# A new order of the same calls on four engines, with 32 more identity transpositions ahead of the first token tiles' work

## What is computed

```
x  [4, 256, 128]                 1024 tokens
1) x = x + attn(layernorm(x))    w_qkv [128, 384]; q and k rms-normed and times ln_w;
                                 16 heads of 8, causal softmax within groups of 32 tokens;
                                 w_proj [128, 128]
2) x = x + xattn(layernorm(x), ctx)
                                 layernorm(gamma, beta); w_q [128, 1024]; ctx [4, 64, 128];
                                 w_kv [128, 2048]; 16 heads of 64, softmax over the 64 context
                                 rows; w_out [1024, 128], b_out; times tanh(gate)
3) x = x + moe(layernorm(x))     router [16, 128] -> sigmoid scores + bias; 2 of 4 groups by
                                 their best two; 4 of 16 experts by top_k; weights normed, x 2.5
                                 each expert: (silu(x Wg) * (x Wu)) Wd, all 128 x 128;
                                 plus 2 shared experts without weights
```

## Time and profile before

| | us |
|---|---|
| median of 3 runs | 195.54 |
| lowest, highest run | 192.97, 196.81 |
| the profiled execution, its own time | 196.71 |
| its span, first to last instruction | 195.20 |
| TensorE busy (matmul) | 177.7 |
| DVE busy | 145.9 |
| POOL busy | 121.7 |
| ACT busy | 116.2 |
| mean granted clock of TensorE | 0.965 |

### The profile page before, as it was taken

One profiled execution on the slowest core, in us unless ns is written; L12 is line 12 of the kernel. 1 busy time (PEld: TensorE's weight loads), 2 busy tenths in 40 slices (PEclk: granted clock), 3 DMA queues, 4 the chain that ended last, 5 costly groups with the idle time before them and its releaser, 6 DMA issues.

```text
span 195.2 us, 4807 instructions
## 1 busy us (share of the span) xinstructions
PE 177.7 (91%) x1671; PEld 127.9 (66%) x1671; DVE 145.9 (75%) x296; ACT 116.2 (60%) x276; POOL 121.7 (62%) x190
## 2 busy tenths in 40 slices
PE   5579999999878999999999989997997999999984
PEld 5345666666545657877787757455765888888863
DVE  2636387868877888888899876999999566756841
ACT  2344778677776678866778677153624663663640
POOL 4726234625671866887978766983966665746670
PEclk9855799999999999999999999999999999999999
DMA  4667000000007029200000006462330066443301
GB/s 121 168 230 200 3 0 7 5 3 3 0 27 195 0 77 291 67 3 2 0 0 3 0 7 199 149 217 72 126 104 0 7 218 178 175 130 108 111 0 54
DMA packets 16983, 15.92 MB, mean 82 GB/s; under 512 B 1841, under 2 KB 12609, under 8 KB 16833
## 3 DMA queue, kind: packets, MB, share of 16 engines
q1 hardware_dynamic: 16672, 15.49, 26.3%
q10 hardware_dynamic: 288, 0.13, 0.2%
HBM read 15.03 MB, written 0.59 MB: 80 GB/s over the span
## 4 chain that ended last, share of the span: by engine, by line
PE 63%; DVE 14%; DMA 6%; issue 5%; ACT 5%; POOL 2%; SPq 2%; DVEq 0%; ACTq 0%; POOLq 0%
PE wide L1771 8%; PE bank L1799 6%; PE wide L1829 5%; PE wide L1830 5%; PE wide L1831 5%; PE bank L1716 4%; DMA wkv_sb<-w_rows 3%; PE bank L1870 3%; PE bank L1871 3%; PE bank L1873 3%; PE wide L1731 3%; DMA wq_sb<-in_L_xattn_w_q_dram 2%; PE bank L1625 2%; PE bank L1785 2%; DVE vbd L1398 2%
## 5 line engine op out<-in xcount | busy, mean ns | idle before, releaser
L627 POOL TENSOR_TENSOR aw_lo<-vbd,aw_hi 128x512 fp32r<-128x512 f32 x26 | 33.4, 1295 | 20.3 <-ACT aw_hi L902 20.1
L886 ACT ACTIVATE kbd<-wide 128x512 f32<-128x512 f32 x36 | 21.4, 598 | 27.2 <-DVE wide L1387 16.3
L1829 PE MATMUL wide<-x3hi,gu_lo 128*128 128x512 f32 x72 | 31.4, 436 | 2.2 <-DVE vbd L1398 1.5
L1830 PE MATMUL wide<-x3lo,gu_hi 128*128 128x512 f32 x72 | 28.6, 397 | 0.0
L1831 PE MATMUL wide<-x3hi,gu_hi 128*128 128x512 f32 x72 | 28.3, 393 | 0.0
L1387 DVE TENSOR_TENSOR wide<-kbd,wide 128x512 f32<-128x512 f32 x27 | 18.5, 689 | 10.6 <-PE wide L1831 7.4
L902 ACT CAST aw_hi<-vbd 128x512 fp32r<-128x512 f32 x26 | 15.8, 617 | 6.4 <-DVE vbd L1398 4.3
L1398 DVE TENSOR_TENSOR vbd<-wide,wkv_sb 128x512 f32<-128x512 f32 x27 | 18.5, 689 | 1.3 <-DMA wkv_sb<-w_rows 0.6
L1829 PEld LDWEIGHTS wide<-x3hi,gu_lo 128*128 128x128 f32 x72 | 13.5, 188 | 8.2 <-issue 3.6
L515 POOL TENSOR_TENSOR p<-p,rs 128x1024 f32<-128x1024 f32 x8 | 15.2, 1903 | 3.6 <-DVE rs L1239 3.6
L1799 PE MATMUL bank<-vo_fold,p2T 128*128 128x128 f32 x128 | 16.7, 280 | 0.5 <-DVE x L1245 0.4
(11 more groups left out here) (176 smaller groups left out, 416.2 us busy)
## 6 DMA issues: line engine op xcount, KB each, us to landing
wkv_sb<-w_rows SPq DMA_DIRECT2D x32, 256.0 KB, 3.2
wkv_sb<-in_L_xattn_w_kv_dram SPq DMA_DIRECT2D x1, 1024.0 KB, 4.8
kv<-in_L_ffn_gate_w_dram SPq DMA_DIRECT2D x4, 256.0 KB, 4.2
kv<-in_L_ffn_up_w_dram SPq DMA_DIRECT2D x4, 256.0 KB, 5.2
wq_sb<-in_L_xattn_w_q_dram SPq DMA_DIRECT2D x1, 512.0 KB, 4.6
wout_sb<-in_L_xattn_w_out_dram SPq DMA_DIRECT2D x1, 512.0 KB, 6.5
wq_sb<-in_L_ffn_down_w_dram SPq DMA_DIRECT2D x1, 512.0 KB, 3.8
wqT<-in_L_ffn_down_w_dram SPq DMA_DIRECT2D x1, 512.0 KB, 5.1
```

Of the source, the lines that this page charges most:

```text
L627: pool.tensor_tensor(aw_lo[:, k % 3, :], weighted_of(k), aw_hi[:, k % 3, :].bitcast(F32), ALU.subtract).then_inc(alo_s, 1)
L886: sc.activation(sil[:, k % 2, :], bank[up_bank(k)], ACT.Silu).then_inc(sil_s, 1)
L1829: pe.matmul(dst, lo, x3hi[:, cols], start=True, stop=False)
L1830: pe.matmul(dst, hi, x3lo[:, cols], start=False, stop=False)
```

## The change

All calls of before stand in the lists of after, each as often as before: 122 calls on POOL, 234 on ACT, 193 on DVE, and 282 on TensorE, with six keep_busy calls added there, which are 2 + 9 + 9 + 6 + 3 + 3 = 32 transpositions. WIDE_TURNS follows TensorE's new order. SyncE's list and all functions are the same. The diff is cut to the parts that are spoken of; in the others neighbours change places in the same way.

TensorE:

```diff
             keep_busy(12)
             transpose_xn(0, 0, T1[:, 0:P])
+            keep_busy(2)
             project_v(0)
             fold(("ctx", 0))
             project_qkv(0)
+            keep_busy(9)
             fold(("wq", 0), halves=(0,))
             fold(("wq", 0), halves=(1,))
+            keep_busy(9)
+            transpose_qk(0)
             fold(("wq", 1))
-            transpose_qk(0)
+            keep_busy(6)
             transpose_xn(0, 1, T1[:, 0:P])
+            keep_busy(3)
             project_qkv(1)
+            scores1(0)
             project_v(1)
-            scores1(0)
             fold(("kv", 0), halves=(0,))
             fold(("kv", 0), halves=(1,))
+            keep_busy(3)
             transpose_qk(1)
             fold_A(0)
             transpose_xn(0, 2, T1[:, 0:P])
             fold(("kv", 1), halves=(0,))
+            fold(("kv", 1), halves=(1,))
             project_qkv(2)
+            scores1(1)
             project_v(2)
             transpose_p1(0)
-            scores1(1)
-            fold(("kv", 1), halves=(1,))
...
             fold_A(7)
-            values1(6)
+            fold_VW(0)
+            project_y(6)
             scores2(0)
-            project_y(6)
             transpose_p1(7)
-            fold_VW(0)
...
             transpose_p2(5, 0)
             scores2(7)
-            transpose_xn(2, 3, T1[:, P:2 * P])
+            gate(0)
             transpose_p2(5, 1)
             logits(3)
+            up(0)
             output2(5, 0)
+            gate(1)
             output2(5, 1)
             transpose_p2(6, 0)
-            gate(0)
-            up(0)
+            up(1)
+            transpose_xn(2, 4, T1[:, P:2 * P])
             transpose_p2(6, 1)
+            logits(4)
+            down(0)
```

ACT:

```diff
             squares(0)
+            scale_qk(0)
             copy_fold(("wq", 0))
-            scale_qk(0)
             copy_qkT(0)
             copy_xnT(1)
+            squares(1)
             copy_fold(("wq", 1))
-            squares(1)
-            gate_tanh()
             scale_qk(1)
...
             copy_p2T(5, 0)
-            copy_x3T(3)
-            split_hi(12)
+            silu(0)
             copy_p2T(5, 1)
             exp_logits(3)
             exp2(7)
             copy_p2T(6, 0)
-            silu(0)
-            split_hi(13)
-            copy_p2T(6, 1)
-            silu(1)
             split_down_hi(0)
             copy_x3T(4)
+            split_hi(10)
+            split_down_hi(1)
+            copy_p2T(6, 1)
+            exp_logits(4)
+            silu(1)
             copy_p2T(7, 0)
+            copy_x3T(5)
+            copy_p2T(7, 1)
             silu(2)
-            exp_logits(4)
-            copy_p2T(7, 1)
-            split_hi(14)
-            copy_x3T(5)
             exp_logits(5)
```

DVE:

```diff
+            zero_vbd()
             norm_stats(0, 0)
             norm_stats(0, 1)
             norm_apply(0, 0)
-            zero_vbd()
+            head_mask()
             norm_stats(0, 2)
             norm_stats(0, 3)
+            norm_apply(0, 1)
+            build_vbd(0)
             norm_stats(0, 4)
...
             softmax2_sub(7)
-            residual2(5)
+            multiply(0)
             biased_scores(0)
             softmax2_sum(7)
+            residual2(5)
+            norm_stats(2, 5)
             group_scores(0)
-            norm_stats(2, 5)
-            multiply(0)
+            residual2(6)
+            norm_stats(2, 6)
             rank_groups(0)
...
             biased_scores(1)
+            group_scores(1)
             multiply(3)
             multiply(4)
-            group_scores(1)
+            rank_groups(1)
             multiply(5)
             weigh(2)
...
             multiply(9)
-            rank_groups(1)
             weigh(9)
```

POOL:

```diff
             build_kbd(0)
-            late_constants()
...
-            scale_bias()
...
-            add_bias()
...
+            norm_apply(1, 4)
+            norm_p2(0)
+            late_constants()
+            scale_bias()
+            norm_scale(1, 6, 1.0 + LN_EPS, LN_EPS * LN_EPS)
             add_bias()
-            norm_scale(1, 4, 1.0 + LN_EPS, LN_EPS * LN_EPS)
-            norm_apply(1, 3)
-            norm_scale(1, 5, 1.0 + LN_EPS, LN_EPS * LN_EPS)
-            norm_scale(1, 6, 1.0 + LN_EPS, LN_EPS * LN_EPS)
             norm_scale(1, 7, 1.0 + LN_EPS, LN_EPS * LN_EPS)
-            norm_p2(0)
...
```

More of the change, by code:

```diff
@@ L672, in _ @@
+            norm_p2(3)
             norm_scale(2, 1, 1.0, LN_EPS)
+            norm_apply(2, 1)
+            split_lo(2)
             norm_apply(1, 6)
-            norm_apply(2, 1)
-            norm_p2(3)
             split_x3(0)
-            norm_p2(4)
             norm_scale(2, 2, 1.0, LN_EPS)
             norm_apply(2, 2)
+            norm_p2(4)
             norm_apply(1, 7)
             split_x3(1)
+            norm_scale(2, 3, 1.0, LN_EPS)
+            norm_apply(2, 3)
             norm_p2(5)
-            norm_scale(2, 3, 1.0, LN_EPS)
@@ L1108, in _ @@
             copy_rows(1)
[L1109 removed]
+            split_act_hi(17)
             silu(20)
[L1111 removed]
             split_act_hi(18)
+            silu(21)
             copy_y(0)
+            silu(22)
             split_act_hi(19)
[L1115 removed]
             split_act_hi(20)
[L1117 removed]
             silu(23)
@@ L1122, in _ @@
             silu(25)
+            silu(26)
             split_act_hi(23)
-            silu(26)
+            silu(27)
             split_act_hi(24)
@@ L1536, in _ @@
             weigh(5)
+            multiply(7)
             weigh(6)
-            multiply(7)
             weigh(7)
@@ L1546, in _ @@
             weigh(10)
+            mask_groups(1)
             multiply(11)
             weigh(11)
-            mask_groups(1)
             multiply(12)
+            choose_experts(1)
+            weigh(12)
             multiply(13)
-            weigh(12)
             weigh(13)
-            choose_experts(1)
             multiply(14)
+            multiply(15)
+            weigh(14)
             chosen_scores(1)
-            weigh(14)
-            multiply(15)
+            multiply(16)
             weigh(15)
-            multiply(16)
+            weigh(16)
             expert_weights(1)
-            weigh(16)
             multiply(17)
@@ L1569, in _ @@
             multiply(21)
+            multiply(22)
             weigh(21)
             add_y()
-            multiply(22)
             weigh(22)
@@ L1922, in _ @@
             fold(("kv", 1), halves=(0,))
+            fold(("kv", 1), halves=(1,))
             project_qkv(2)
+            scores1(1)
             project_v(2)
             transpose_p1(0)
-            scores1(1)
-            fold(("kv", 1), halves=(1,))
+            fold_A(1)
+            fold(("kv", 2), halves=(0,))
             values1(0)
             transpose_qk(2)
-            fold(("kv", 2), halves=(0,))
+            fold(("kv", 2), halves=(1,))
+            transpose_xn(0, 3, T1[:, 0:P])
             project_y(0)
-            transpose_xn(0, 3, T1[:, 0:P])
-            fold_A(1)
+            transpose_p1(1)
             project_qkv(3)
@@ L2089, in _ @@
             up(5)
+            gate(7)
+            gate(8)
             up(6)
-            gate(7)
             up(7)
-            gate(8)
             down(2)
@@ L2101, in _ @@
             up(9)
+            down(6)
+            up(10)
             gate(11)
-            down(6)
             gate(12)
-            up(10)
+            up(11)
             down(7)
-            up(11)
+            up(12)
+            gate(13)
             down(8)
-            gate(13)
-            up(12)
+            gate(14)
             up(13)
-            gate(14)
             down(9)
@@ L2115, in _ @@
             up(14)
+            down(10)
+            up(15)
             gate(16)
-            down(10)
             down(11)
-            gate(17)
-            up(15)
-            gate(18)
             down(12)
@@ L2182, in _ @@
             down(33)
+            gate(35)
             down(34)
```

432 lines of the change are left out of this document (211 added, 221 removed), and 6 rows, old and new, of the table WIDE_TURNS.

## The result

The changed kernel takes **193.71 us** (median of 11 runs, 193.12 to 194.76) against 195.54 (192.97 to 196.81) for the kernel before in the same comparison. The ratio is 0.994, with a 95% interval from 0.9912 to 0.9968: faster by 0.6%, or some 1.2 us. The ratio leaves out as slow the three runs of before that took over 1.5% more than its fastest (195.92, 196.46 and 196.81 us); the two medians alone are 1.8 us apart, and what follows goes by ratios. The forecast was 192.5 us, 3.0 us or 1.6% less than before. The sign is right and the time lies in the range, but of the 3.0 us the ratio shows 1.2.

The account below looks back on a forecast made before the run. TensorE was taken to bound most of the kernel, with a half-clock dip in the head, and DVE from 99 to 150 us. Sum: 196.71 - 3.8 - 0.6 + 1.3 - 1.1 = 192.5 us, range 189.0 to 197.0.

Parts of the forecast that it names:

- Together -3.8 us: TensorE's head: transpositions keep the clock full; fold_A(0) 2.4 us earlier, 1.4 us more up to the kv 1 half.
- the walk: New order of the head followed at warm durations from the wq transpositions at 8.40 us to fold_A(0) at about 16.0.
- Perhaps the quick run kept its clock: Guess that the 192.97 us run of before held full clock; runs differ by 3.8 us, the clock term's worth.
- the clock falls all the same: Rival: half clock from 8.4 to 22 us, dummies cost 3.2 us and give nothing back; 199.5 us, chance 0.12.
- zero_vbd() at the head: DVE's head: first tile's norm 0.1 to 0.4 us later, hidden by the wq DMA; taken 0.
- The fold order: Around 57 us: fold_VW(0) ahead of scores2(0) fills TensorE's idle gaps; -0.6 us, bounds 0 and -1.1.
- POOL's bias: add_bias behind norm_p2(0), ready before output2(0) with 0.5 to 2.5 us cover; taken 0, bounds 0 and +0.5.
- ACT's tables: Five exp/silu switches instead of three, exp2(7) 3.2 us and routing 2.4 us late; +1.3 us, bounds 0 and +3.8.
- The second routing: rank_groups(1) moved into DVE's wait for the weight rows before 121.12 us; -1.1 us, bounds 0 and -3.3.
- the order is worth more: Rival: filled waits in the DVE-bound stretch give their upper bounds, loads half hidden; 189.2 us, chance 0.26.

Follow-up runs that it names:

- the head alone: New order with the 32 transpositions up to about 78 us, the order of before from there, against before: 1.004, median 196.34 us.
- the execution above with 1.0: Profiled execution of before with only group_scores(1) moved ahead of multiply(3) and rank_groups(1) ahead of multiply(5); timed at 0.9951 of before, median 194.31 us.
- The head without the 32: New order without the 32 transpositions up to about 78 us, the order of before from there, against before: 1.0017, median 195.96 us.
- the tail alone: Order of before without new transpositions up to about 78 us, the new order from there, against before: 0.9963, median 194.22 us.
- the one move in before: Before with group_scores(1) moved ahead of multiply(3) and rank_groups(1) ahead of multiply(5) on DVE, against before: 0.9951, median 194.31 us.
- one more call in DVE's wait: Changed kernel without the 32 transpositions, with mask_groups(1) moved right behind rank_groups(1), against before: 0.9839, median 192.23 us.

## Why the prediction was right or wrong

**The clock and the 32 transpositions: the step that failed.** It is the line "Together -3.8 us". That the 32 would hold the clock was right in all four executions that have them. But the lead at the mark was 1.98 us and not 3.8 (1.6 in the mean of all executions), and the timed kernels keep nothing of it that can be measured: 0.994 with the transpositions and 0.9934 without, 1.0017 for the new head without them and 1.004 with them. Three things were wrong in it.

The first is that a lead in the head was taken for time at the end. In the head alone, with the 32, the walk came true: fold_A(0) started at 16.05 us and the lead at the mark was 2.44 us. It was still 2.46 us at the second store of weight rows, 0.62 us at the loads behind it and 0.6 us at the end (below: "What gave lead back later").

The second is the base. I took 196.71 us, the profiled execution, for my sum, though "the median of the runs is 195.54, 1.2 less than the profiled one" stands in it, and I put the difference down to the clock term instead of taking it off. The lead of 0.6 us against a trace that was 1.2 us slow is how the head alone can come out at 1.004. I can't say how long the timed runs of before were at half clock in the head. Before was timed 87 times beside the experiments, with mean granted clocks from 0.965 (6 runs, median 196.66 us) over 0.974 (15, 195.75), 0.982 (11, 194.56) and 0.991 (13, 194.44) to 1.0 (37, 195.27), and 5 runs with other values. But the execution above with 1.0 had a cold head up to 21.9 us, and the changed kernel's 0.991 comes from a dip at 112 us: the mean doesn't tell of the head. Of these, the two lowest clocks go with the slowest runs, the highest doesn't go with the fastest. "Perhaps the quick run kept its clock" isn't borne out, and isn't settled either.

The third is the walk's start, in the changed kernel. It gave the nine behind project_qkv(0) 1.0 us and put their end at 7.75, ahead of the wq DMA. They ran from 8.16 at the half pace and ended at 9.9, so the wq transpositions began 1.5 us later than in the earlier trace rows, and 2.4 later than in the execution with the old head and the new tail. Fillers that are meant to keep an engine warm are part of a queue: where it is cold nevertheless they cost double, in front of the work they should help. That this isn't the whole of it the head alone shows, whose nine ran at 0.11 us apiece.

**The rival "the clock falls all the same".** Its condition didn't come (the clock was full from 9.71 us in the stretch of 8.4 to 22 that decides it), and neither did its price. A rule of the Trainium skill had spoken for it ("TensorE: Matmul & The Clock Gate", Part 4: PE-mode transpose, the full clock doesn't engage for transposes). The runs don't bear it out as a rule: the twelve identity transpositions from 2 us were the only work before full clock at 4.79 us in the execution with the new head alone; in before it came at 4.91, with the transposition of tile 0 from 4.76 besides. They aren't a reliable trigger either: with the same twelve, the clock rose only at 9.71 in the changed kernel and at 18.20 with the old head and the new tail. What decides it isn't shown by any run here.

**zero_vbd() at the head.** Taken: 0. The transposition of tile 0 came at 5.41 us where it was 4.76: 0.65 us late, and not 0.1 to 0.4. project_qkv(0) came at 7.31 for 6.16, but 0.55 of these 1.15 us aren't zero_vbd's: in the head alone, with the same zero_vbd() and the 32 and a clock at full, it came at 6.76. It's one reason why the nine started only at 8.16. Whether it costs time in the end stays open (0.989 with it moved back, overlapping).

**The fold order.** Taken: -0.6. The head without the 32, which has it, doesn't beat before (1.0017). No run isolates the move of fold_VW(0); nothing shows the 0.6, and 0 is nearer.

**POOL's bias.** Taken: 0, and right: add_bias starts at 67.77 and ends at 69.03, output2(0, 0) starts at 71.21. The cover is 2.2 us, in the range of 0.5 to 2.5.

**ACT's tables.** Taken: +1.3. There are five loads, as said, and the tail alone loses 1.9 us up to the last routing step and 1.1 at the weight rows. The size holds, but not by the path I gave: exp2(7) started at 97.69 us against 98.88, which is 0.8 us late against the lead of 1.98 and not 3.2, and the routing began at 97.83 against 99.32, 0.5 us late and not 2.4 (1.4 in the tail alone). That the loads alone are the loser is argued, since other neighbours changed there too; the experiment that was to price them changed TensorE's waits instead.

**The second routing.** Taken: -1.1. Two measurements isolate it: 0.49% from the one move in before (1.0 us), and 0.69% between the new order without the 32 with and without it (0.9934 against 1.0003, 1.3 us). The term was right, the waits it named moved as said, and it is the whole of the measured gain: without it (and without the 32) the ratio is 1.0003.

**What gave lead back later.** The changed kernel stores the second set of weight rows 4.16 us earlier than the trace of before, and then DVE waits 3.43 us for their loads (155.55), where before waited 0.56. At the end 3.1 us of lead are left. SyncE's DMA queue shows it, in before, in the changed kernel and in the one with the new head alone:

```profile
152.67 1.72 SPq L447 DMA_DIRECT2D w_rows<-w_rows_sb  x4
...
155.43 1.76 SPq L441 DMA_DIRECT2D wkv_sb<-w_rows  x4
```

```profile
148.51 2.57 SPq L447 DMA_DIRECT2D w_rows<-w_rows_sb  x4
...
152.12 1.76 SPq L441 DMA_DIRECT2D wkv_sb<-w_rows  x4
```

```profile
150.21 1.71 SPq L447 DMA_DIRECT2D w_rows<-w_rows_sb  x4
...
154.81 1.77 SPq L441 DMA_DIRECT2D wkv_sb<-w_rows  x4
```

From the first store to the first load it was 2.76 us in before, 3.61 in the changed kernel and 4.60 with the new head alone: a store 2.46 us earlier gave loads only 0.62 us earlier. That is where most of its 2.44 us of lead at the mark went; the old order with the 32 lost 0.90 us in the same place (3.66 us).

What the record shows beside it is a packet of the DMA queue that the profile calls "instruction", 16 KB and about 1 us long. DMA queues of the new head alone from 152.4 to 153.8 us, and of before from 152.6 to 157.2, all of its stretch from store to load:

```profile
q8 instruction: 1, 0.02, 5.5%
q1 hardware_dynamic: 32, 0.01, 3.3%
```

```profile
q1 hardware_dynamic: 195, 0.17, 12.7%
```

5.5% of 16 engines in 1.4 us are 1.2 us of one of them. The slowest store took 3.3 us to land there, and 1.9 in before. In all four executions with the 32 such a packet starts between the first store of these rows and their last load (149.7 to 152.5 us), and each loses 0.85 to 1.84 us there: three between store and load, the fourth (zero_vbd() moved back) in the loads, which take 2.68 us where they took 1.76. In the nine usable ones without the 32 it starts only after these loads (157.3 us or later) and nothing is lost. So added instructions seem to shift the moment at which the program's own code is loaded, here onto the store that matters. That the packet is the cause is argued from this coincidence; no run moved it alone.

**The rival "the order is worth more".** It named the right stretch, and the change didn't reach it. With one more call in DVE's wait, and without the 32, the time is 192.23 us. That this is near the forecast of 192.5 is luck: it comes by another way than the forecast took.

## What to carry to other kernels

Before a stall in one trace gets a price, look at the same stretch in other executions, and by the pace of the instructions: a mean granted clock of 1.0 hid a cold head here. A lead at an early mark isn't time yet; follow it to the places where engines meet, since instructions added at the head can move something else, here, it seems, the code's own loading. A chain of tiny steps on the engine that sets the pace belongs into a wait of that engine: two moved calls gave 0.5%. A third gave nothing in the old order (0.9952 after 0.9951), where POOL was busy beside it, and 1% in the new one (0.9839 after 0.9934), where POOL was idle; that POOL makes the difference is likely from the step lengths, not isolated. Fillers for the clock stand in the queue ahead of real work; count them at the slow pace.

## What the runs showed of the hardware

**Tiny DVE steps last as long as POOL's instruction beside them.** cmp_a (128x64) took 1.31 us from 130.75 in before and ended at 132.06. The timeline of POOL in before has

```profile
130.65 1.33 POOL L627 TENSOR_TENSOR aw_lo<-vbd,aw_hi 128x512 fp32r<-128x512 f32 x1 [0.95 <-ACT aw_hi L902]
```

which ends at 131.98. A pair of 0.92 and 1.29 us was shown above (ends 119.51 and 119.48). With POOL idle the same forms take 0.22 and 0.17. The Trainium skill, "SBUF — State Buffer", Who interferes with whom, says that a DVE instruction with two SBUF inputs contends with a GpSimd instruction that reads SBUF, that the shared ports are an exclusive lock, and that the order of issue decides who blocks. cmp_a has two inputs in SBUF and started 0.10 us behind POOL's instruction, and in both pairs the ends lie less than 0.1 us apart, as this says; the step of 0.92 us has one, and for tensor_scalar the same section names a mode of its own that takes both ports, which no row here shows. I had read the 1.31 us as the step's own length; beside an idle POOL it takes 1.1 us less.

**The clock of TensorE isn't the same from run to run.** One order of instructions gave mean granted clocks from 0.965 to 1.0, and one timed run of the new head alone had 0.858 and took 204.53 us, where its others took 194.92 to 197.14. One profiled execution, that of the new order without the 32, took 280.57 us with a granted clock of 0.56 from 18 us to its end, while its timed runs lie between 192.78 and 194.86. Its page's slices:

```profile
PEclk9985555555555555555555555555555555555555
```

Only six calls fewer set that kernel apart from the changed one, and no other execution had such a clock. What caused it isn't shown, and no other line of this trace was used.
